# Routed rows of a top-2 expert layer in 25 blocks of 256 and 21 blocks of 128 rows

## What is computed

```python
shared = new_gelu(xf @ Wfc_s + bfc_s) @ Wproj_s + bproj_s          # xf: 4096 x 256, hidden 1024
probs = softmax(xf @ Wr); topk_p, topk_i = top_k(probs, 2); topk_p /= sum(topk_p)
gate = zeros((4096, 8)); gate[row, topk_i] += topk_p
for e in range(8):
    h = new_gelu(xf @ Wfc[e] + bfc[e]) @ Wproj[e] + bproj[e]
    routed = routed + h * gate[:, e:e + 1]
out = x + shared + routed
```

## Time and profile before

| | us |
|---|---|
| time, median of 3 runs | 941.33 |
| lowest and highest | 940.80, 943.58 |
| the profiled execution, its time | 941.67 |
| its span, first to last instruction | 939.9 |

### The profile page before, as it was taken

One profiled execution on the slowest core, in us unless ns is written; L12 is line 12 of the kernel. 1 busy time (PEld: TensorE's weight loads), 2 busy tenths in 40 slices (PEclk: granted clock), 3 DMA queues, 4 the chain that ended last, 5 costly groups with the idle time before them and its releaser, 6 DMA issues.

```text
span 939.9 us, 21652 instructions
## 1 busy us (share of the span) xinstructions
PE 801.1 (85%) x6791; PEld 673.8 (72%) x6791; DVE 631.3 (67%) x2006; ACT 356.6 (38%) x777; POOL 236.3 (25%) x221
## 2 busy tenths in 40 slices
PE   3999999998569610199999999999999999999995
PEld 2666766666358400088888888888888888888884
DVE  4579888988579400088888666666666666666663
ACT  4554554454244200045555333333333333333331
POOL 2211011101100677400000133333333333333333
...
DMA packets 168045, 98.07 MB, mean 104 GB/s; under 512 B 110316, under 2 KB 163336, under 8 KB 167944
## 3 DMA queue, kind: packets, MB, share of 16 engines
...
...
## 4 chain that ended last, share of the span: by engine, by line
PE 60%; issue 20%; another core or an unknown queue 8%; DVE 6%; DMA 2%; ACT 1%; POOL 1%; SPq 1%; POOLq 0%; DVEq 0%; ACTq 0%
PE bank_st L1163 10%; PE bank_kv L1175 10%; PE bank_st L1161 10%; PE bank_kv L1177 10%; PE bank_st L1162 10%; PE bank_kv L1176 10%; DMA stage_w<-in_L_ffn_Wfc_s 1%; POOL rstd L518 1%; DVE w_parts L959 1%; DVE expert_buffers L971 1%; DVE w_parts L738 0%; DMA expert_buffers<-rows_by_expert 0%; DVE expert_buffers L972 0%; DVE stats L827 0%
## 5 line engine op out<-in xcount | busy, mean ns | idle before, releaser
L695 ACT ACTIVATE expert_buffers<-bank_st,bias_columns 128x256 f32<-128x256 f32 x440 | 208.5, 474 | 422.8 <-DVE expert_buffers L972 218.9
L971 DVE TENSOR_SCALAR expert_buffers<-expert_buffers 128x256 f16<-128x256 f32 x440 | 128.8, 293 | 199.4 <-ACT expert_buffers L695 127.2
L1175 PE MATMUL bank_kv<-w_parts,expert_buffers 128*128 (+1 forms) x880 | 241.4, 274 | 1.7 <-DVE expert_buffers L972 1.7
L1177 PE MATMUL bank_kv<-w_parts,expert_buffers 128*128 (+1 forms) x880 | 241.3, 274 | 0.0
L1176 PE MATMUL bank_kv<-w_parts,expert_buffers 128*128 (+1 forms) x880 | 241.3, 274 | 0.0
L972 DVE SCALAR_TENSOR_TENSOR expert_buffers<-expert_buffers 128x256 f16<-128x256 f32 x440 | 188.3, 428 | 15.1
L1161 PE MATMUL bank_st<-expert_buffers,w_parts 128*128 128x256 f16 x624 | 170.1, 273 | 1.4 <-DMA expert_buffers<-rows_by_expert 1.4
L1162 PE MATMUL bank_st<-expert_buffers,w_parts 128*128 128x256 f16 x624 | 170.1, 273 | 0.0
L1163 PE MATMUL bank_st<-expert_buffers,w_parts 128*128 128x256 f16 x624 | 170.1, 273 | 0.0
L1161 PE MATMUL bank_st<-w_parts 128*128 128x256 f16 x256 | 71.9, 281 | 73.2 <-issue 51.3
L561 POOL DMA_INDIRECT out<-expert_buffers,token x78 | 121.8, 1561 | 20.6 <-issue 20.3
...
## 6 DMA issues: line engine op xcount, KB each, us to landing
...
```

The source lines that it names most:

```text
L695: act.activation(g32[f % 2], hid[f % 2][:, 0:BLK], ACT.Gelu_apprx_tanh, bias=bias, scale=UNSCALE).then_inc(s["gelu_done"], 1)
L971: chain(dve.tensor_scalar(g[:, 0, :], g32[f % 2], A_SCALE, None, ALU.mult), "g_hi", c + 1)
L1175: pe.matmul(y, g[:, 0, tile(t)], w_hi, start=f == 0 and t == 0, stop=False, skip_group_check=True)
L1177: op = pe.matmul(y, g[:, 1, tile(t)], w_hi, start=False, stop=f == FC - 1, skip_group_check=True)
```

## The change

The routed rows are laid out in FULL = 25 blocks of 256 rows and HALF = 21 blocks of 128 rows. An expert's rows fill as many whole blocks of 256 as they can (25 in all over the experts, in order), and what is left goes into blocks of 128. That is 71 tiles of 128 rows where there were 78, in 46 blocks where there were 39.

In a block of 128 rows (a half): `up` has the same 6 matmuls per chunk, each with 128 moving columns; gelu, g_hi and g_lo work on 128 columns. `down` is two matmuls: g_hi as the weights against the high and the low part of w2 side by side (512 columns, into two sums of 256), and g_lo against the high part (256 columns). The evacuation is three dependent instructions of 256 columns: y = sum0 x UNSCALE + b2, a wait, y = sum1 x UNSCALE + y, a wait, y x gate. There is one add to the output instead of two. Waits on `y_added` count tiles (`sent`).

The routing has 20 parts instead of 16 and so reaches into block 4; SP's and POOL's loops of the routed stage are written out.

```diff
-    NRT = 2 * T // BLK + E - 1
+    FULL = (2 * T - E * (BLK - 1) + BLK - 1) // BLK
+    HALF = 2 * T // P + E - 1 - FULL * TB
+    NRT = FULL + HALF
     NBLK = NSH + NRT
+    ROW_TILES = FULL * TB + HALF
...
+    PAD_STEPS = (ROW_TILES + PADS * TB - 1) // (PADS * TB)
+    assert FULL == 25 and HALF == 21 and PAD_STEPS < B
...
+    def rows_of(n):
+
+        first = n * BLK if n < FULL else FULL * BLK + (n - FULL) * P
+        return slice(first, first + tiles_in(n) * P)
+
+    def sent(n):
+
+        return sum(tiles_in(m) for m in range(n)) * 16
...
+        xT_half = [x.rearrange("p l k n -> p (l k n)")[:, 0:512].rearrange("p (l k n) -> p l k n", k=DK, l=2) for x in xT]
...
+        def width(G):
+            return P * tiles_in(G - NSH)
...
                 sp.wait_ge(s["meta_taken"], n)
-                sp.dma_start(meta, tiles_of(rows_dram, n)[:, :, D:ROW]).then_inc(s["meta_loaded"], 16)
...
+                sp.dma_start(meta[:, 0:tiles_in(n), :],
+                             rows_dram[rows_of(n), D:ROW].rearrange("(t p) w -> p t w", p=P)).then_inc(s["meta_loaded"], 16)
+
+            def load_xT(n):
+
+                if n >= 2:
                     sp.wait_ge(s["up_done"], FC * (n + (NSH - 1)))
-                sp.dma_start_transpose(xT[parity].rearrange("p l k n -> p (l k) n"),
-                                       rows16_dram[ds(n, 1)].rearrange("a r w -> (a r) w")).then_inc(s[f"xT_loaded{parity}"], 16)
+                dst = xT[n % 2] if n < FULL else xT_half[n % 2]
+                sp.dma_start_transpose(dst.rearrange("p l k n -> p (l k) n"),
+                                       rows16_dram[rows_of(n), :]).then_inc(s[f"xT_loaded{n % 2}"], 16)
 
...
-            with sp.Fori(0, NRT // 2 - 1) as j:
-                for c in range(2):
-                    load_xT(2 * j + (2 + c), c)
-                    load_b2(2 * j + (1 + c + NSH), expert_of(2 * j + (1 + c)))
-                    if c == 0:
-                        load_rows(2 * j + 3)
-                    else:
-                        load_rows(2 * j + 4)
-            load_xT(NRT - 1, (NRT - 1) % 2)
-            load_b2(NRT - 2 + NSH, expert_of(NRT - 2))
+            for n in range(NRT - 2):
+                load_xT(n + 2)
+                load_b2(n + (1 + NSH), expert_of(n + 1))
+                if n + 3 < NRT:
+                    load_rows(n + 3)
             load_b2(NRT - 1 + NSH, expert_of(NRT - 1))
...
-                    pool.wait_ge(s["y_added"], n * (16 * TB))
+                    pool.wait_ge(s["y_added"], sent(n))
 
                 pool.tensor_tensor(carrier[:, :], minus_half[:, 0:1], minus_half[:, 0:1], ALU.add)\
                     .then_inc(s["carried"], 1)
-                for t in range(TB):
+                for t in range(tiles_in(n)):
                     pool.indirect_dma_start(
                         out=out_rows, out_offset=bass.IndirectOffsetOnAxis(ap=token[slot][:, t:t + 1].bitcast(U32), axis=0),
                         in_=ybuf[slot % 2][:, t, :], in_offset=None, bounds_check=last_token, oob_is_err=False,
                         compute_op=ALU.add).then_inc(s["y_added"], 16)
...
-                    act.activation(g32[f % 2], hid[f % 2][:, 0:BLK], ACT.Gelu_apprx_tanh, bias=bias,
+                    w = width(G)
+                    act.activation(g32[f % 2][:, 0:w], hid[f % 2][:, 0:w], ACT.Gelu_apprx_tanh, bias=bias,
                                    scale=UNSCALE).then_inc(s["gelu_done"], 1)
...
                 elif part == 5:
-                    then(dve.tensor_scalar(nblk_i, upto[:, :, TILES - 1], float(BLK - 1), None, ALU.add))
-                    then(dve.tensor_scalar(nblk_i2, nblk_i, BLK.bit_length() - 1, None, ALU.logical_shift_right))
-                    then(dve.tensor_copy(nblk, nblk_i2))
+                    then(dve.tensor_copy(count_i, upto[:, :, TILES - 1]))
+                    then(dve.tensor_scalar(nfull_i, count_i, BLK.bit_length() - 1, None, ALU.logical_shift_right))
+                    then(dve.tensor_copy(nfull, nfull_i))
                 elif part == 6:
-                    then(dve.tensor_tensor_scan(blk_end, ones_e, nblk, 0.0, ALU.mult, ALU.add))
-                    then(dve.tensor_tensor(first_row, blk_end, nblk, ALU.subtract))
+                    then(dve.tensor_tensor_scan(full_sum, ones_e, nfull, 0.0, ALU.mult, ALU.add))
+                    then(dve.tensor_tensor(full_first, full_sum, nfull, ALU.subtract))
+                    dve.tensor_scalar(full_end, full_sum, float(FULL), None, ALU.min)
+                    then(dve.tensor_scalar(full_first, full_first, float(FULL), None, ALU.min))
                 elif part == 7:
-                    dve.tensor_tensor(base, upto, totals, ALU.subtract)
+                    then(dve.tensor_tensor(full_rows, full_end, full_first, ALU.subtract))
+                    then(dve.tensor_scalar(full_rows, full_rows, float(BLK), None, ALU.mult))
+                    then(dve.tensor_tensor(rest, upto[:, :, TILES - 1], full_rows, ALU.subtract))
+                    then(dve.tensor_scalar(rest_i, rest, float(P - 1), None, ALU.add))
                 elif part == 8:
-                    then(dve.tensor_tensor(past, iota_blk.rearrange("p (n a) -> p n a", a=1).broadcast_to([P, NRT, E]),
-                                           blk_end.rearrange("p (a e) -> p a e", a=1).broadcast_to([P, NRT, E]),
+                    then(dve.tensor_scalar(nhalf_i, rest_i, P.bit_length() - 1, None, ALU.logical_shift_right))
+                    then(dve.tensor_copy(nhalf, nhalf_i))
+                    then(dve.tensor_tensor_scan(half_end, ones_e, nhalf, 0.0, ALU.mult, ALU.add))
+                    then(dve.tensor_tensor(half_first, half_end, nhalf, ALU.subtract))
+                elif part == 9:
+                    then(dve.tensor_tensor(past[:, 0:FULL, :],
+                                           iota_blk.rearrange("p (n a) -> p n a", a=1).broadcast_to([P, FULL, E]),
+                                           full_end.rearrange("p (a e) -> p a e", a=1).broadcast_to([P, FULL, E]),
                                            ALU.is_ge))
-                elif part == 9:
+                elif part == 10:
+                    then(dve.tensor_tensor(past[:, FULL:NRT, :],
+                                           iota_blk[:, 0:HALF].rearrange("p (n a) -> p n a", a=1).broadcast_to([P, HALF, E]),
+                                           half_end.rearrange("p (a e) -> p a e", a=1).broadcast_to([P, HALF, E]),
+                                           ALU.is_ge))
+                elif part == 11:
                     then(dve.tensor_reduce(blk_f, past, AX.X, ALU.add))
                     dve.tensor_scalar(blk_expert[:, :], blk_f, float(E - 1), None, ALU.min)
-
-                elif part == 10:
+                    then(dve.tensor_scalar(full_rows, full_end, float(BLK), None, ALU.mult))
+
+                elif part == 12:
+                    then(dve.tensor_tensor(base, upto, totals, ALU.subtract))
                     then(dve.scalar_tensor_tensor(
-                        base, first_row.rearrange("p (e a) -> p e a", a=1).broadcast_to([P, E, TILES]), float(BLK),
+                        base, full_first.rearrange("p (e a) -> p e a", a=1).broadcast_to([P, E, TILES]), float(BLK),
                         base, ALU.mult, ALU.add))
-                elif part == 11:
+                elif part == 13:
+                    then(dve.scalar_tensor_tensor(jump, half_first, float(P), full_rows, ALU.mult, ALU.subtract))
+                    then(dve.tensor_scalar(jump, jump, float(FULL * BLK), None, ALU.add))
                     then(dve.tensor_tensor(place, te(count_ps[:, 0, :]), base.rearrange("p e t -> p t e"), ALU.add))
-                elif part < 16:
-                    j = (part - 12) // 2
+                elif part == 14:
+                    then(dve.tensor_tensor(beyond, place, over_t(full_rows), ALU.is_ge))
+                elif part == 15:
+                    then(dve.tensor_tensor(beyond, beyond, over_t(jump), ALU.mult))
+                    then(dve.tensor_tensor(place, place, beyond, ALU.add))
+                else:
+                    j = (part - 16) // 2
                     if part % 2 == 0:
                         then(dve.tensor_tensor(chosen, place, hot[j], ALU.mult))
                     else:
                         then(dve.tensor_reduce(dest_f[:, j, :], chosen, AX.X, ALU.add))
-                    if part == 15:
+                    if part == 19:
                         dve.tensor_copy(dest[:, :, :], dest_f).then_inc(s["routed"], 1)
...
-                        dve.wait_ge(s["y_added"], (16 * TB) * (G - (NSH + 1)))
+                        dve.wait_ge(s["y_added"], sent(G - (NSH + 1)))
+                if G >= NSH + FULL:
+                    y = ybuf[parity][:, 0, :]
+                    chain(dve.scalar_tensor_tensor(y, ysum[parity][:, 0, :], UNSCALE, b2blk, ALU.mult, ALU.add),
+                          "y_part", G - (NSH + FULL) + 1)
```

(33 more changed lines are left out.)

55 lines of the change are left out of this document (31 added, 24 removed).

## The result

The changed kernel takes 944.6 us (median of 14 runs, 941.8 to 946.5) against 940.9 for the kernel before in the same runs (14 runs, 937.0 to 944.0): a ratio of 1.0040, with a 95% interval of 1.0026 to 1.0053. The forecast was 942 us and no difference that can be measured. The time is inside its range, and the small loss, 3.75 us, is real.

A forecast was written before the change was run, and what follows sets the result against it. PE bounds the routed stage before; in half blocks DVE's stops and a chain through the engines would. 941.67 - 0.1 + 0.6 - 2.6 + 2.8 = 942.4 profiled, so 942 us, no measurable difference; range 930 to 962.

The forecast's parts named there:

- PE stops being the bound in half blocks: Half blocks: DVE alone needs 5.7 us against PE's 5.28, so the 36 us saved by columns bring nothing.
- Durations carried to 128 columns: Half blocks: gelu 0.37, g_hi 0.23, g_lo 0.30, a matmul 0.056 us, extrapolated from other lengths.
- the rival that gave 953: Half blocks' `up`: weight loads show at 0.098 us per matmul, half block 7.5, time 953; chance 0.11.
- The chain L: Half blocks: from g(c) through down(c), up(c + 3) and gelu to g(c + 3), 2.05 us for three chunks.
- The copies' path: Half blocks: DVE's gate and row copies at f = 6 hold g(7) by 0.77 us; with two L, period 6.97.
- PE's own register load: Half blocks: PE's load of the expert, 0.51 us and at most as much again, hidden behind g(7), costed at nothing.
- Where PE waits: Half blocks: PE's idle time ends with g_lo, ahead of `down` of f = 3, 6, 7 and 2.
- Sum of the stage: Routed stage: 25 x 10.46 + 21 x 6.97 = 408.0 us against 408.1, plus 0.6 for the first half block.
- Tail: Kernel's end: one scatter-add fewer saves 1.55 + 0.30, a shorter last chunk about 0.8; -2.6 us.
- Routing: Shared blocks 1 to 4: more DVE routing instructions than PE's time hides, +2.8 us.
- PE or DVE alone as the bound: Half blocks: PE alone 5.3 to 5.6 us, DVE without the chain 5.7 to 6.5; 907 to 932; chance 0.13.
- if nothing stopped: Scatter in the shared blocks: without the engines' stop up to 75 us gone; scatter rival's chance 0.06 to either side.

The follow-up runs named there:

- e1: In half blocks PE reads the next block's expert after `up` of f = 5, against the changed kernel; 866.0 us, ratio 1.0012 to the kernel before.
- e5: The changed kernel unaltered, run again beside other runs on a chip with the scatter's stop; 946.0 us, ratio 1.0054 to the kernel before (940.8).

## Why the prediction was right, and where it was not

- *PE stops being the bound in half blocks, and the gain is gone.* Right. PE is shown busy for 83% in the half blocks (forecast about 75%; by the starts of its matmuls its own work is 5.28 of 7.20 us, 73%). Of the 36 us that the stage would save by its columns nothing is left: it takes 4.7 us longer.
- *Durations carried to 128 columns.* Right throughout: gelu 0.37 (forecast 0.37), g_hi 0.22 or 0.23 (0.23), g_lo 0.29 (0.30), evacuation 850.05 to 851.23 = 1.18 (1.16), `up` and `down` together 0.66 (0.66). Full blocks take 10.48 (10.46). That a matmul of 128 columns costs 0.056 and the weight load doesn't show is settled: the rival that gave 953 is refuted. The Trainium skill's 81 ns for that pair (TensorE: Matmul & The Clock Gate, Back-to-back issue gap) doesn't hold here, where six matmuls, each with its own weights, take 0.33 us (852.26 to 852.59).
- *The chain L and the period.* The copies' path was sized right: 6.96 to 6.97 in e1, forecast 6.97. The step that failed is "PE's own register load ... lies behind the g(7) that is held by the copies, so I cost it at nothing". The load comes before the copies' g(7) is wanted, right behind `down(5)`, and delays gelu(0) to gelu(2), and with them the next evacuation. Its size, "up to 0.7", came near (0.76); it was set against the wrong cover. The loop through PE's queue was never added up: with the forecast's own terms it is (1.16 + 0.56 + 0.13) + 2 x 0.66 + 2 x 0.33 + 0.66 + 0.33 + 1.04 + 0.47 = 6.33 and the load. With the load's row alone (0.51) that is 6.84 and under the other path, with 0.7 it is 7.03 and over it, with "as much again" 7.35. The sum would have shown two loops of nearly the same length, and that the load can't be put at nothing. From 7.03 the rest of the 7.19 is the long g_hi (0.08), the load's 0.76 in place of 0.7, and 0.02 of rounding.
- *Where PE waits.* Forecast: ahead of `down` of f = 3, 6, 7 and 2, each time until g_lo ends. Seen: ahead of `down(3)` until g_lo ends, and ahead of up(0), where the load is. That sign failed in three of its four places, and it was the one that told of the wrong path while the period still lay inside its bounds.
- *Sum of the stage.* 408.0 + 0.6 was forecast, 412.8 measured: +4.2, of which 20 periods x 0.23 make 4.6.
- *Tail.* -2.6 forecast, -3.2 measured.
- *Routing.* +2.8 at the scatter, 2.4 measured; evacuations 11.9 and 11.3 apart in blocks 1 and 2 were forecast, 11.5 and 12.4 are seen: the sum comes out near and its split doesn't. At the start of the routed stage the kernel is only 1.4 us behind. Compared gelu by gelu, it is 1.56 behind from f = 5 of block 6, just after the stop, to the end of the shared blocks. So about 0.8 of the 2.4 goes within the stop, and no run looked into why.
- *Together.* 942.4 forecast for the profiled execution, 944.6 measured: -1.4 at the start of the stage, +4.2 in it, -0.6 in the tail, which is 2.2. That the time came out nearer than the routed stage is luck: two errors of the other sign stand beside it. The term of the half block alone is what turned no difference into a small loss. It lies inside the bounds given for it (6.7 to 7.2).
- *The other rivals.* PE or DVE alone as the bound (5.3 to 6.5 us) is refuted by the 7.20. The clock is 1.00 in the half blocks. DVE's evacuations don't wait for the adds. The scatter's stop has the same length, 90.2 against 89.7 us, on this chip; 90.6 in e5. On the two chips without it some 75 us are gone (865.6 and 865.9 against 940.8), as the forecast had it for "if nothing stopped", but for the kernel before as well.
